# A gated cross-attention block on one core: 36 cyclic pairs per head in place of 48, batches innermost

## What is computed

```python
kv  = einsum('bhil,bhjl->bijhl', k_, v_)            # k = v = context: all products of two channels of a head
y   = irfft(rfft(kv, 2L) * rfft(ssm_kernel, 2L))[..., :L] + kv * D   # a causal convolution along l, per head
out = einsum('bijhl,bhil->bjhl', y, q_)             # q = layernorm(x)
x   = x + tanh(g_xattn) * out
z   = layernorm(x)                                  # then a mixture of experts: 8 experts, the best 2 by a softmax router
x   = x + tanh(g_ffn) * (sum_e gate_e * gelu(z @ expert_w[e] + b_e) @ out_w + out_b)
```

## Time and profile before

| | us |
|---|---|
| median of three executions (121.16 to 122.09) | 121.27 |
| the profiled execution | 121.62 |
| its span in the trace | 119.8 |
| PE busy in the span | 108.2 |
| DVE busy | 92.8 |
| POOL busy | 66.6 |
| ACT busy | 55.8 |

### The profile page before, as it was taken

One profiled execution on the slowest core, in us unless ns is written; L12 is line 12 of the kernel. 1 busy time (PEld: TensorE's weight loads), 2 busy tenths in 40 slices (PEclk: granted clock), 3 DMA queues, 4 the chain that ended last, 5 costly groups with the idle time before them and its releaser, 6 DMA issues.

```text
span 119.8 us, 1978 instructions
## 1 busy us (share of the span) xinstructions
PE 108.2 (90%) x622; PEld 94.3 (79%) x622; DVE 92.8 (77%) x274; ACT 55.8 (47%) x138; POOL 66.6 (56%) x103
## 2 busy tenths in 40 slices
PE   4957999999686999695999999999999999999981
PEld 4946999999576899592788888885788888888970
DVE  0288699999976999999958878587698766867851
ACT  4134109365023362651866996954372441443420
POOL 3059993586999999959999989960000000000000
PEclk9999999999999999999999999999999999999998
DMA  3768999591002202002000000000000110011121
GB/s 97 260 190 224 341 351 334 144 281 40 0 0 88 88 5 90 1 0 84 9 0 0 0 3 0 0 0 5 0 0 0 44 44 0 0 44 49 44 87 47
DMA packets 9916, 8.97 MB, mean 75 GB/s; under 512 B 1290, under 2 KB 9906, under 8 KB 9906
## 3 DMA queue, kind: packets, MB, share of 16 engines
q1 hardware_dynamic: 8530, 7.80, 21.2%
q10 hardware_dynamic: 1376, 1.05, 2.8%
HBM read 7.77 MB, written 1.07 MB: 74 GB/s over the span
## 4 chain that ended last, share of the span: by engine, by line
PE 55%; POOL 16%; DMA 15%; SPq 7%; issue 3%; ACT 1%; DVE 1%; POOLq 0%
PE ring L783 13%; PE ring L785 12%; PE ring L784 12%; POOL kv_t L363 6%; DMA rwlast<-in_L_ffn_router_w 6%; POOL kv_t L366 4%; POOL w_lo_t L417 3%; PE red L730 3%; DMA kpad_dram<-mix_t 3%; PE red L754 3%; DMA ctx_t<-in_L_ffn_expert_b 2%; DMA dcol<-in_L_xattn_D 2%; SPq L324 2%; DMA ctx_t<-in_L_ffn_expert_w 2%; SPq L319 2%
## 5 line engine op out<-in xcount | busy, mean ns | idle before, releaser
L1004 DVE SCALAR_TENSOR_TENSOR mix_t<-ring,gates_t,mix_t 128x256 f32<-128x256 f32 x55 | 26.4, 483 | 6.8 <-ACT ring L571 5.3
L571 ACT ACTIVATE ring<-ring 128x512 f32<-128x512 f32 (+1 forms) x33 | 18.8, 568 | 18.1 <-PE ring L785 18.1
L783 PE MATMUL ring<-w_hi_t,zT_hi_t 128*128 128x512 f32 (+1 forms) x66 | 26.8, 406 | 0.0
L785 PE MATMUL ring<-w_hi_t,zT_lo_t 128*128 128x512 f32 (+1 forms) x66 | 25.5, 386 | 0.0
L784 PE MATMUL ring<-w_lo_t,zT_hi_t 128*128 128x512 f32 (+1 forms) x66 | 25.4, 385 | 0.0
L363 POOL TENSOR_TENSOR kv_t<-ctxT_t 128x256 f32<-128x256 f32 x23 | 16.3, 710 | 5.4 <-ACT ctxT_t L486 5.4
L704 PE MATMUL ring<-kv_t,toep_t 128*128 128x192 f32 x64 | 16.2, 334 | 3.4 <-POOL kv_t L366 2.6
L705 PE MATMUL ring<-kv_t,toep_t 128*128 128x192 f32 x64 | 15.6, 326 | 0.0
L706 PE MATMUL ring<-kv_t,toep_t 128*128 128x192 f32 x64 | 15.6, 326 | 0.0
L909 DVE TENSOR_TENSOR zq_t<-ring,qT_t 128x256 f32<-128x256 f32 x32 | 13.2, 412 | 2.2 <-PE ring L706 2.0
L785 PEld LDWEIGHTS ring<-w_hi_t,zT_lo_t 128*128 128x128 f32 x66 | 12.4, 188 | 2.7
(11 more groups left out here) (114 smaller groups left out, 188.2 us busy)
## 6 DMA issues: line engine op xcount, KB each, us to landing
ctx_t<-in_L_ffn_expert_w SPq DMA_DIRECT2D x8, 256.0 KB, 2.7
toep_t<-kpad_dram SPq DMA_DIRECT2D x3, 512.0 KB, 6.3
wlast_t<-in_L_ffn_expert_w SPq DMA_DIRECT2D x1, 1024.0 KB, 10.0
out<-x_t SPq DMA_DIRECT2D x8, 128.0 KB, 1.7
ctx_t<-in_ctx ACTq DMA_DIRECT2D x2, 256.0 KB, 3.1
x_t<-in_x ACTq DMA_DIRECT2D x2, 256.0 KB, 3.8
ctx_t<-in_ctx SPq DMA_DIRECT2D x2, 256.0 KB, 3.8
x_t<-in_x SPq DMA_DIRECT2D x2, 256.0 KB, 7.4
```

The source lines that it names most:

```text
L571: act.activation(y, y, ACT.Gelu_apprx_tanh).then_inc(gelu_ready, 1)
L783: pe.matmul(y, hi, whi, start=(c == 0), stop=False)
L785: last = pe.matmul(y, lo, whi, start=False, stop=(c == C - 1))
L1004: dve.scalar_tensor_tensor(out=acc, in0=ring[n % RING][:, L * e:L * (e + 1)], scalar=gate, in1=acc, op0=ALU.mult, op1=ALU.add).then_inc(mi ...
```

## The change

**Pairs.** The products of a head are indexed by distance: for d = 0 to 3 all eight pairs (i, i+d), wrapping around, and for d = 4 four pairs, 36 in all. They are made in two instructions of 256 and 32 elements. To let a window of 8 channels slide past the end, `ctxT_t` and `qT_t` hold 11 channels per head, the first 3 a second time; each copy out of PSUM has a second, shorter instruction for them.

**Layout.** In `ctxT_t`, `qT_t`, `kv_t` and `zq_t` the 8 (chunk, batch) come innermost. The convolution reads and writes 36 runs of 4 elements, 144 columns in place of 192, 8 elements apart. Transpositions into PSUM write elements 4 apart, and the sums read their operand 8 elements apart. The read-out is four instructions of 256, 192, 32 and 32 elements.

**x twice.** The rows of x are loaded into the still unused half of `zq_t` for statistics and queries, and again into `x_t`, channels permuted, for the residual; the output is written back through the same permutation.

**Folds.** Halving batch by batch goes. Group 0 is summed from all 8 terms (64 transpositions). For group 1 four folds (1024 elements, all batches at once) add terms 4 to 7 to terms 0 to 3, two on DVE and two on POOL; every sum of the group waits for all four.

**Order.** `kv_t` has 6 slots. The sums of group 0 stand behind steps 18 to 21, those of group 1 behind blocks 3 to 6. Only two batches are transposed before block 0; the other two and the router's logits come behind block 0, and `route_rows` behind block 1. The first three expert weights are asked for ahead of the router's bias, and the preparations stand at POOL's steps 13, 17 and 21.

```diff
-SLOTS = 8
+SLOTS = 6
 RAW = 4
 LOADS = 4
 TOEP = ((0, 1), (1, 3), (4, 4), (8, 4), (12, 4))
-BY_VECTOR = (0, 8, 13, 15, 18, 23, 24, 28, 30)
-HALVED_BY_DVE, HALVED_BY_POOL = (1, 2, 3, 4, 5), (6, 7)
+BY_VECTOR = (0, 4, 7, 10, 13, 16, 19, 22, 25, 28)
+FOLDED = (0, 4)
 WARM_UP = (12, 1, 6, 1, 5, 5)
-SUMS = (16, 18, 19, 21)
-HALVES = (15, 15, 17)
-ZTS = (27, 29, 30, 31)
-ROUTER_SPLIT = 27
-X_SCALES, X1_SCALES = 13, 27
+SUMS = (18, 19, 20, 21)
+ZTS = (30, 31)
+ROUTER_SPLIT = 21
+X_SCALES, X1_SCALES = 12, 31
 ROUTER_REL = 15
-WREL = (16, 18, 24, 29)
-LATE_SUMS = (1, 2, 3, 4)
-LATE_SPLIT = 5
-LATE_ZTS = (10, 10, 12, 12)
+WREL = (13, 17, 21)
+EARLY = 3
+RAW_SPLITS = (0, 1, 3, 7, 8)
+LATE_SUMS = (3, 4, 5, 6)
+LATE_ZTS = (11, 11, 12, 12)
...
-    NP = HD * HD - HB * HB
-    NPU = HB * HD
+    ND = HB * HD
+    NP = ND + HB
+    HX = HD + HB - 1
...
+        xn = zq_t[:, CB * HD * P:CB * HD * P + B * L].rearrange("p (b l) -> p b l", b=B)
+        ctxT = ctxT_t[:, :].rearrange("p (g h i a) -> p g h i a", g=G, h=H, i=HX)
+        qT = qT_t[:, :].rearrange("p (g h i a) -> p g h i a", g=G, h=H, i=HX)
+        kv = kv_t[:, :].rearrange("p (s n a) -> p s n a", s=SLOTS, n=NP)
...
+        zq = zq_t[:, :].rearrange("p (g i n a) -> p g i n a", g=G, i=HD, n=P)
...
+        def by_channel(src, b):
+            return bass.AP(src.tensor, b * S * L, [[L, HD], [HD * L, H], [1, L]])
...
+        def windows(tensor, g, h):
+            return bass.AP(tensor, (g * H + h) * HX * CB, [[G * H * HX * CB, P], [CB, HB], [1, HD * CB]])
...
+        def last_rows(sp, e, n):
+            src = bass.AP(expert_w.tensor, e * L * L + (L - 1) * L, [[0, P], [L * L, n], [1, L]])
+            sp.dma_start(wlast[:, e:e + n, :], src).then_inc(last_rows_in, 16)
...
+                if i >= len(TOEP) - 3 and i < len(TOEP) - 1:
+                    load(sp, xn, x, x_in, i - len(TOEP) + 5)
+            last_rows(sp, 0, EARLY)
             sp.dma_start(rw, router_w.rearrange("(c p) n -> p c n", c=C)).then_inc(router_in, 16)
             sp.dma_start(rwlast[:, :], everywhere(router_w, (L - 1) * E, E)).then_inc(router_in, 16)
+            sp.wait_ge(context_transposed, B // BL)
+            for e in range(EARLY):
+                raw_weights(sp, e)
+            sp.wait_ge(router_in, 32)
+            sp.dma_start(rw_t[P - 1:P, E:2 * E], router_b.rearrange("(a n) -> a n", a=1)).then_inc(router_bias_in, 16)
+            for e in range(EARLY):
+                raw_bias(sp, e)
+            for b in range(BG):
+                sp.dma_start(xv[:, b, :], by_channel(x, b)).then_inc(x_rows_in[b], 16)
+            last_rows(sp, EARLY, E - EARLY)
             sp.dma_start(obias[:, :], everywhere(out_b, 0, L)).then_inc(out_bias_in, 16)
             sp.dma_start(ow, out_w.rearrange("(c p) n -> p c n", c=C)).then_inc(out_weights_in, 16)
-            sp.wait_ge(router_in, 32)
-            sp.dma_start(rw_t[P - 1:P, E:2 * E], router_b.rearrange("(a n) -> a n", a=1)).then_inc(router_bias_in, 16)
-            sp.wait_ge(context_transposed, B // BL)
-            for e in range(RAW):
-                raw_weights(sp, e)
-            for e in range(RAW):
-                raw_bias(sp, e)
-            raw_weights(sp, RAW)
-            for e in range(RAW + 1, E):
+            raw_weights(sp, EARLY)
+            for b in range(BG, B):
+                sp.dma_start(xv[:, b, :], by_channel(x, b)).then_inc(x_rows_in[b], 16)
+            for e in range(EARLY + 1, E):
                 raw_weights(sp, e)
                 raw_bias(sp, e - 1)
             raw_bias(sp, E - 1)
             for b in range(B):
                 sp.wait_ge(y_ready, b + 1)
-                sp.dma_start(out[b], xv[:, b, :]).then_inc(results_out, 16)
+                sp.dma_start(by_channel(out, b), xv[:, b, :]).then_inc(results_out, 16)
...
+            head = ctxT[:, g, h].rearrange("p i a -> p (i a)")
+            dst = kv[:, n % SLOTS].rearrange("p n a -> p (n a)")
+            eng.tensor_tensor(dst[:, 0:ND * CB].rearrange("p (d i) -> p d i", d=HB),
+                              head[:, 0:HD * CB].unsqueeze(1).to_broadcast([P, HB, HD * CB]), windows(ctxT_t, g, h),
+                              ALU.mult)
+            eng.tensor_tensor(dst[:, ND * CB:NP * CB], head[:, 0:HB * CB], head[:, HB * CB:HD * CB],
+                              ALU.mult).then_inc(done, 1)
+        def fold(eng, g, i, done):
+            eng.wait_ge(read_out, (g + 1) * H)
+            terms = zq[:, g].rearrange("p i n a -> p i (n a)")
+            eng.tensor_tensor(terms[:, i], terms[:, i], terms[:, HB + i], ALU.add).then_inc(done, 1)
...
-                for i in due(WREL, n - 2):
+                for i in due(WREL, n - 4):
...
+            fold(pool, 1, 2, pool_folded)
             weights_low(first)
-            halve_sum(pool, HALVED_BY_POOL[1], pool_halved)
+            fold(pool, 1, 3, pool_folded)
             weights_low(first + 1)
-            for e in range(first + 2, E):
+            relative(first + 2)
+            weights_low(first + 2)
+            for e in range(first + 3, E):
...
+            def evacuate(dst, banks, ready, g, c, done):
+                act.wait_ge(ready, (g + 1) * BG // BL)
+                src = banks[c][:, :].rearrange("p (h i b) -> p h i b", h=H, i=HD)
+                own = dst[:, g, :, :, BG * c:BG * (c + 1)]
+                act.activation(own[:, :, 0:HD], src, ACT.Copy).then_inc(done, 1)
+                act.activation(own[:, :, HD:HX], src[:, :, 0:HX - HD], ACT.Copy).then_inc(done, 1)
...
-                if j == LATE_SPLIT:
-                    for e in range(len(WREL) + 2, E):
-                        split_weights(e)
+                for i in due(LATE_SUMS, j - 1):
+                    statistics(B + BG + i)
+                for i in due(RAW_SPLITS, j):
+                    split_weights(len(WREL) + i)
                 if j == 0:
-                    split_weights(len(WREL))
+                    route(0)
                 if j == 1:
                     route_gates(0)
-                    split_weights(len(WREL) + 1)
-                    statistics(B + BG)
+                if j == 2:
+                    scale_bias()
+                    projection_high()
...
+                y = ring[n % RING][:, 0:NP * CB].rearrange("p (n a) -> p n a", a=CB)
+                src = kv[:, n % SLOTS]
+                first, second = slice(0, BG), slice(BG, CB)
+                within, past = toep[:, h, P:2 * P], toep[:, h, 0:P]
+                pe.matmul(y[:, :, first], within, src[:, :, first], start=True, stop=True)
+                pe.matmul(y[:, :, second], past, src[:, :, first], start=True, stop=False)
+                pe.matmul(y[:, :, second], within, src[:, :, second], start=False, stop=True).then_inc(convolved, 1)
...
-                n = HD
-                if b in HALVED_BY_DVE:
-                    pe.wait_ge(dve_halved, HALVED_BY_DVE.index(b) + 1)
-                    n = HB
-                if b in HALVED_BY_POOL:
-                    pe.wait_ge(pool_halved, HALVED_BY_POOL.index(b) + 1)
-                    n = HB
+                if g:
+                    pe.wait_ge(dve_folded, 2)
+                    pe.wait_ge(pool_folded, 2)
+                slots = [i for i in range(HD) if not HB <= i < HB + FOLDED[g]]
                 for c in range(C):
-                    for i in range(n):
-                        last = pe.matmul(red[b % 2][:, P * c:P * (c + 1)], zq[:, g, BG * c + b % BG, i, :], ident[:, :],
-                                         is_transpose=True, start=(i == 0), stop=(i == n - 1))
+                    for i in slots:
+                        last = pe.matmul(red[b % 2][:, P * c:P * (c + 1)], zq[:, g, i, :, BG * c + b % BG], ident[:, :],
+                                         is_transpose=True, start=(i == 0), stop=(i == slots[-1]))
...
+                if n < BG:
+                    pe.wait_ge(z_low_ready, b + 1)
...
-            route_logits(0)
             for j, (b, k) in enumerate(BLOCKS):
                 experts(j, b, k)
                 for i in due(LATE_SUMS, j):
...
                 for i in due(LATE_ZTS, j):
                     z_transposed(BG + i)
                 if j == 0:
+                    for i in range(2, BG):
+                        z_transposed(i)
+                    route_logits(0)
+                if j == 1:
...
+                y = ring[n % RING][:, 0:NP * CB]
+                pairs = y[:, 0:ND * CB].rearrange("p (d i a) -> p d i a", d=HB, i=HD)
+                far = y[:, ND * CB:NP * CB].rearrange("p (i a) -> p i a", i=HB)
+                q = qT[:, g, h]
+                def terms(first, outer, inner, count):
+                    at = (g * HD * P + h + first) * CB
+                    return bass.AP(zq_t, at, [[G * CB * HD * P, P], *outer, [inner * CB, count], [1, CB]])
+                dve.tensor_tensor(terms(HB * P, [[P * CB, HB]], H, HD), pairs,
+                                  windows(qT_t, g, h).rearrange("p d (i a) -> p d i a", i=HD), ALU.mult)
```

(10 more changed lines are left out.)

136 lines of the change are left out of this document (40 added, 96 removed).

## The result

The changed kernel takes **122.61 us** (median, 122.01 to 122.93), the kernel before beside it 121.69 (121.15 to 122.55). The ratio is 1.007, with a 95% interval of 1.0038 to 1.0102: about 0.9 us slower, where 119.0 was predicted. The trace of after is of a run of 122.01 us, the quickest of its set; its span is 120.2 us, for 119.8 before.

A forecast was written before the change was run, and what follows sets the result against it. The prediction took PE to bound the experts and POOL the stretch from 28 to 47 us; 121.62 - 2.9 gained by block 4 + 0.2 for the output store = 118.9, stated as 119.0 us, range 117.0 to 124.2.

The forecast's parts named there:

- the first rival: Sums, operands 8 elements apart: a transposition takes 0.163 us, not 0.109, adding 5.2 us on PE: 124.2 us; chance 0.20.
- DVE as the bound of the steps: Convolution steps: DVE needs 1.01 us a step against PE's 0.74, so PE's saved 7.7 us is mostly not collected.
- The bias no longer late: Router's bias DMA that POOL waits for: predicted to land at 23.5 us, bounds 22.5 and 28.
- The piece up to product 18: POOL's work from the bias landing through product 18, before convolution 18: 7.2 us in all, delivered at 30.7.
- The start: Products wait for four context copies, not two: first read-out goes from 13.96 to 14.9 us.
- the steps' DVE products: DVE's product in every third step: 0.43 us alone plus 0.2 lost to POOL, so 0.63.
- PE sets this piece: Sums of group 0: 64 transpositions, 7.0 us, with three convolutions of 0.74 between, ending at 40.4 us.
- this mark: Block 4's start with three of group 1's four sums done: 62.6 us for 65.53, a gain of 2.9.
- the end: Output rows written permuted in DRAM: 0.2 us added, bounds 0 and 0.4.
- The stall moves along and is not gained: Logits moved behind block 0: the low part's stall of 1.20 us before stands behind block 0 instead, with no gain.
- the late bias: Rival: router's bias lands at 26 us, giving 121.4 us, or at 28, giving 123.5 with POOL the bound; chance 0.13.
- the convolutions at 0.325: Rival: convolutions keep their 0.325 us, costing about 1.8 us: 120.8 us, no change; chance 0.10.

The follow-up runs named there:

- the experiment: Changed kernel with ScalarE's splits of the last two experts' weights earlier and POOL's low parts ahead of the last normalisation's scales: 122.33 us, 1.0020 to the kernel before.
- the second trace of the changed kernel: Trace of the changed kernel timed again with nothing changed, as common base of the experiments: 122.64 us, 1.0065 to the kernel before.

## Why the prediction was wrong, point by point

**Right.** A convolution product at 0.245 us; a transposition at 0.111, so the first rival is dead; the read-out at 0.80; DVE as the bound of the steps, which the experiments with less PE and more DVE work both show. The bias no longer late: POOL begins its piece at 22.37, without a wait. That was partly luck. The piece up to product 18 took 8.2 us (22.37 to 30.57) and not 7.2, since a product on POOL cost 0.87 and not 0.77 and the router's two subtractions (0.33) were left out; the bias, predicted at 23.5, came early enough to pay for it. From block 0 to block 4: 11.24 us for 11.3 predicted, with the fold's wait behind block 3 (0.97 for 1.1). The start: predicted was a first read-out at 14.9; nine of the traces above with this start unchanged give 14.66 to 15.21, mean 14.91, and the result's own, with 14.32, was the lucky one.

**Wrong: the steps' DVE products.** "Between 0 and 0.34 I take 0.2, so 0.63" a product. The five of group 0 took 0.73, 0.75, 0.43, 0.65 and 1.25 us, 0.66 more in all, and that of step 22 took 1.96; the last two lie far outside the bounds (0.43 to 0.77). The error is in the kind of price: 0.34 was a mean over nine products, and the trace shows no even slowing. Seven of DVE's ten products met a product, a weight subtraction or `weights_low` on POOL. In all seven the first instruction ended 0.28 to 0.29 us after POOL's, and the second, of 32 elements, 0.04 to 0.06 us after it: a product pays what is left of its neighbour. The traces of the variants show the same distances, and so do nearly all such products in the kernel before (0.27 to 0.29 for 256 elements), so its trace held this price already. The three others took 0.43 or 0.44, among them that of step 0, which met only the last 0.06 us of one. The 1.25 met two subtractions, the 1.96 `weights_low` (1.28 us) and a product. The read-outs beside the same work kept their 0.41, so it is not all of DVE's work that is held up. The 1.96 also broke "PE sets this piece", which held only as long as the residuals were on time: the third sum waited for one. The ends are read from the trace; one case was forced by experiment: moving the product of step 22 brings back 0.8 to 1.0 us. Block 0 came at 51.48 for 49.6, **1.9 us** late, the largest miss: 0.3 of it by the end of convolution 18 (31.47 for 31.2, although the first read-out was 0.6 early), 1.0 from there to the end of convolution 22 (10.9 us for 9.9; the third sum starts 0.7 late), and 0.6 behind it (9.1 for 8.5), where product 28 took 0.91.

**Wrong: what comes after block 4.** "PE is full from there, so what this mark gains, the kernel gains." From the mark (62.72 + 1.74 = 64.46) to the last addition's end it is 52.73 us, before from 65.53 to 117.70 it was 52.17: **0.56** lost. Half of it (0.25 to 0.3) is block 12's wait for the last low parts, by the experiment. The starts of the blocks place the rest: two sums between blocks cost 1.85 us and not the mark's 1.74, and block 13 starts 2.12 us behind block 12, for 1.74 before (from block 8 to block 14 it is 11.26 us, for 10.78). From block 14 to the end nothing is lost (34.90 for 34.93). What holds block 13 up was not tested.

**Wrong: the end.** 0.2 was taken, with 0.4 as the bound; by the tails it is **0.86** in the changed kernel (3.04 for 2.18) and 0.94 in the kernel before (3.04 for 2.10). The bound counted bytes at a rate, and the price lies in the issue (0.27 of it) and behind it. The Trainium skill's rule (DMA: Bandwidth & Descriptors, Why a DMA increments its semaphore by 16 and not by 1), on how many engines serve a transfer with a slowest dimension of 8, pointed the right way; a store with a slowest dimension of 16 recovers only 0.3, so it explains about a third.

At the mark behind block 4 1.83 of the 1.9 were left (a gain of 1.07 us for 2.9). 1.8 + 0.6 + 0.7 (a tail 0.9 longer than before's, for 0.2) = 3.1 us is the distance from the predicted 118.9 to the traced run of 122.01. The other 0.6 to the median goes with the start: 14.91 on average, 14.32 in that trace. That is read from traces; no experiment forced it.

**Counted as nothing, and worth something.** "The stall moves along and is not gained": putting the logits back into the changed kernel costs 2.0 to 2.8 us, about half of it by the clock, and 1.2 in the quickest run. That is not a gain over the kernel before, which had one wait of 1.20 ahead of block 0 and a clock of 1.00 there (54 to 58 us). It did not enter the sum, which was made step by step for the new order, but the parts of the change are of opposite sign: this one helps, the output's permutation costs 0.9.

**Of the rivals** none came as written. The strided operands' price, the late bias and the convolutions at 0.325 did not occur. The slower side was reached by something not on the list: DVE and POOL in each other's way on the path, and the store.

## What to carry to other kernels

When an engine becomes the new bound, price its instructions not alone but beside what its neighbour then runs. Here a mean slowing of 0.34 us hid that one product could wait for the whole of a 1.28 us instruction. Look for the one whose lateness is passed on: here a product that stood in front of a residual. A permuted layout has to be undone somewhere, and at the very end nothing hides it: count the issue and landing of the last transfer as part of the path. Side work that several consumers wait for (here a fold) gained 1.2 us by standing in DVE's idle time ahead of the choice and not behind it.

## What the runs showed of the hardware

- A store of 128 rows of 1 KB was issued in 0.33 us with its rows in order, in 0.54 as 16 groups of 8 and in 0.60 as 8 of 16; from the last addition to the end of the span these gave 2.18, 2.74 and 3.04 us. Half of the rows took 0.55 on the same queue, and 1.39 on ACT's, which had not been used since the start.
- Weight loads of PE with 8 elements from one to the next took longer, and the transposition hardly did (0.111 us for 0.109). Loads for transpositions whose operand lay in a row kept 140 to 141 ns in the changed kernel. The group of weight loads after, against 141 ns in the earlier trace rows (busy us, mean ns, idle before):

```profile
L736 PEld LDWEIGHTS red<-ident,zq_t 128*128 128x128 f32 x96 | 11.6, 192 | 2.4 <-issue 1.4 <-DVE x_t L940 0.8
```

- This bears on the Trainium skill's rules on lines of 16 bytes in SBUF and on patterns with gaps in PSUM (Advanced Engine Details and Errata, Memory Cachelines): at this spacing the longer load stayed hidden. On PSUM the trace does not agree with it: convolutions written in runs of 4 elements, 8 apart, took 0.245 us, and 0.244 follows from the columns alone; two transpositions written 4 elements apart took 0.22 (26.64 to 26.86).
- A DVE product of 256 elements with both operands in SBUF took 0.41 us alone and 1.43 beside POOL's `weights_low`; one of 32 elements 0.18 alone and up to 0.71 beside POOL. It ended when POOL's instruction had (0.28 to 0.29 and 0.04 to 0.06 us after it). Read-outs, with one operand in PSUM, took 0.41 either way.
- The granted clock fell to 0.50 in the start of some traces (after PE had stood 2.22 us for the context's third load in the second trace of the changed kernel, but not after 2.31 in the first); twice in the steps without a third of the products (0.66 on average of the stretch shown, and 0.50 at the first sum); and behind the three bare waits ahead of block 0.
